# Four graph layers: copies of k, v and q of the next group ahead of the table copies, q requested behind the tables, output weights loaded during the sums

## What is computed

```python
def _typed_matmul(x, W, node_type):                 # one weight matrix per node type (4 types)
    all_t = jnp.einsum('ni,tio->tno', x, W)
    return all_t[node_type, jnp.arange(x.shape[0])]
k = _typed_matmul(h, k_linears, node_type).reshape(n, N_HEADS, D_K)      # 4 heads of 64
q = _typed_matmul(h, q_linears, node_type).reshape(n, N_HEADS, D_K)
v = _typed_matmul(h, v_linears, node_type).reshape(n, N_HEADS, D_K)
q_att = jnp.einsum('nhd,rhde->rnhe', q, relation_att)                    # 8 relations
v_msg = jnp.einsum('nhd,rhde->rnhe', v, relation_msg)
attn_score = jnp.sum(q_att[etype, col_idx] * k[row_idx], axis=-1)
score = attn_score * (relation_pri[etype] / SQRT_DK)
...
agg = jax.ops.segment_sum(alpha[..., None] * v_msg[etype, row_idx], col_idx, num_segments=n)
out = _typed_matmul(agg, a_linears, node_type)
out = jax.nn.sigmoid(skip)[node_type][:, None] * out
```

## Time and profile before

| | |
|---|---|
| time, median of 3 runs | 4174.1 us (4173.09 to 4183.92) |
| profiled execution, its own time | 4177.06 us |
| span of that execution | 4175.2 us |
| busy: PE, DVE, ACT, POOL | 75%, 54%, 21%, 66% |
| mean granted TensorE clock | 0.846 |
| group loop of the tables | about 1686 to 1936 |
| edges, first gather | 1952 |
| output, first instruction | 2966 |

### The profile page before, as it was taken

One profiled execution on the slowest core, in us unless ns is written; L12 is line 12 of the kernel. 1 busy time (PEld: TensorE's weight loads), 2 busy tenths in 40 slices (PEclk: granted clock), 3 DMA queues, 4 the chain that ended last, 5 costly groups with the idle time before them and its releaser, 6 DMA issues. The chain is left out here.

```text
span 4175.2 us, 64203 instructions
## 1 busy us (share of the span) xinstructions
PE 3149.1 (75%) x11666; PEld 2153.8 (52%) x11666; DVE 2234.4 (54%) x7572; ACT 894.9 (21%) x2584; POOL 2743.4 (66%) x2879
## 2 busy tenths in 40 slices
PE   5999938777788873786788878888786776767763
PEld 2444426556566652333667767777544444444442
DVE  8200037666666646333788868776654433444435
ACT  1333300000200000342344456555320000100000
POOL 3777767777677775234777767777217777477774
PEclk9999959999999986998887769877888877788876
DMA  4333323333333334566555546555213333333332
GB/s 142 142 145 151 142 73 105 106 105 105 95 105 106 106 107 131 217 257 233 165 165 165 164 129 176 163 162 162 66 50 106 105 105 106 99 106 105 105 106 90
DMA packets 226896, 540.00 MB, mean 129 GB/s; under 512 B 73482, under 2 KB 107948, under 8 KB 212876
## 3 DMA queue, kind: packets, MB, share of 16 engines
q0 software_dynamic: 136528, 374.97, 30.1%
q1 hardware_dynamic: 57880, 103.46, 6.8%
q10 hardware_dynamic: 32164, 57.91, 4.7%
HBM read 390.04 MB, written 146.09 MB: 128 GB/s over the span
## 5 line engine op out<-in xcount | busy, mean ns | idle before, releaser
L604 POOL DMA_INDIRECT gcn_edges_g<-table,rows_i x782 | 740.3, 947 | 434.3 <-ACTq L875 196.7
L923 PE MATMUL ps<-gcn_edges_g,gcn_edges_onehot 128*128 x1760 | 627.8, 497 | 309.1 <-SPq L620 271.4
L969 DVE TENSOR_TENSOR acc<-acc,ps 128x256 f32 (+1 forms) x880 | 370.0, 420 | 750.6 <-PE ps L923 740.3
L923 PEld LDWEIGHTS ps<-gcn_edges_g,gcn_edges_onehot 128*128 128x128 f32 x1760 | 392.2, 242 | 537.3 <-issue 484.5
L307 POOL DMA_INDIRECT records<-rec,slots x391 | 375.9, 961 | 184.1 <-issue 124.2
L604 POOL DMA_INDIRECT score_g<-table8v,rows_i x391 | 380.2, 972 | 131.0 <-issue 110.6
L604 POOL DMA_INDIRECT rel_g<-table,rows_i x391 | 371.8, 951 | 134.7 <-issue 96.9
L604 POOL DMA_INDIRECT score_g<-table8k,rows_i x391 | 371.4, 950 | 135.0 <-issue 109.4
L604 POOL DMA_INDIRECT conv_edges_g<-table,rows_i x391 | 371.7, 951 | 127.3 <-issue 93.8
L359 PE MATMUL ps<-w,xt 128*128 128x512 f32 x1000 | 435.8, 595 | 18.3 <-ACT xt L329 18.3
L1047 PE MATMUL ps<-q,onehot_t 128*128 x880 | 322.8, 503 | 109.6 <-DVE onehot_t L1146 108.3
(11 more groups left out here) (319 smaller groups left out, 4768.6 us busy)
## 6 DMA issues: line engine op xcount, KB each, us to landing
table<-tb SPq DMA_DIRECT2D x50, 1280.0 KB, 4.5
score_dst_bc<-dst_rows ACTq DMA_DIRECT2D x110, 256.0 KB, 3.5
sum_dst_bc<-dst_rows ACTq DMA_DIRECT2D x110, 256.0 KB, 3.4
gcn_edges_g<-table,rows_i POOLq DMA_INDIRECT x782, 2.8
table<-gcn_tb SPq DMA_DIRECT2D x50, 128.0 KB, 1.7
records<-rec,slots POOLq DMA_INDIRECT x391
rel_g<-table,rows_i POOLq DMA_INDIRECT x391, 2.8
conv_edges_g<-table,rows_i POOLq DMA_INDIRECT x391, 2.8
```

The source lines that it names most:

```text
L604: pool.indirect_dma_start(out=m.g[:, 2 * slot_of(p) + j, 0:D], out_offset=None, in_=table, in_offset=bass.IndirectOffsetOnAxis(ap=m.rows_i ...
L923: mm = pe.matmul(bank(m, i % BANKS, 0, width), m.onehot[:, 2 * k + j, :], window(m.g, slot + j, 0, width), start=(j == 0), stop=(j == 1))
L969: nc.vector.tensor_tensor(acc, acc, bank(m, i % BANKS, 0, width), ALU.add).then_inc(added, 1)
```

## The change

In `attention_tables`, ACT copies k and v of group i+1 before its table copies of group i, and `pick(i+2)` moves behind the kvt copy of i. DVE copies q of group i+1 before its table copies of group i. `pick` waits for a part of `xs` only when it comes to the first group that may need it. The read of `q_rows` is issued after both tables have landed; SP doesn't wait for it, PE does, at the start of the edges. The output weights are read into `m.q` by SP between the scores and the sums of the edges; `w_a` and its load in the output stage are gone, and PE reads the weights from `m.q`.

```diff
@@ attention_scores, tensor
         regs = ItemRegisters(pe, m, "score")
+        pe.wait_ge(m.q_back, 16)
         for i in range(total):
@@ attention_edges
             scores[0](sp)
+            sp.wait_ge(q_spread, ITEMS)
+            for ty in range(NTYPES):
+                sp.dma_start(m.q[:, 0:2 * NTYPES, :].rearrange("p (k t) d -> p k t d", t=NTYPES)[:, :, ty, :],
+                             a.a_lin[ty].rearrange("(k p) d -> p k d", p=P)).then_inc(m.out_weights, 16)
             sums[0](sp)
@@ attention_tables, sync
+            for j in (0, 1):
+                sp.wait_ge(stored[j], 16 * G)
             for b in (0, 1):
                 sp.wait_ge(q_slots[b], 16 * (G // 2))
-            sp.dma_start(m.q[:, 0:NT, :], m.q_rows[0:ROWS, :].rearrange("(t p) d -> p t d", p=P)).then_inc(q_stored, 16)
-            sp.wait_ge(q_stored, 16)
-            for j in (0, 1):
-                sp.wait_ge(stored[j], 16 * G)
+            sp.dma_start(m.q[:, 0:NT, :], m.q_rows[0:ROWS, :].rearrange("(t p) d -> p t d", p=P)).then_inc(m.q_back, 16)
@@ attention_tables, scalar
             def pick(i):
                 if i < G:
+                    if i < NT and i % PART == 0:
+                        act.wait_ge(back[i // PART], 16)
                     ...
+            def keep_kv(i):
+                if i < G:
+                    act.wait_ge(typed, i + 1)
+                    if i >= 2:
+                        act.wait_ge(kv_turned, i - 1)
+                    copy(kv[:, i % 2, :], bank(m, 1, 0, 512)).then_inc(kv_ready, 1)
...
-            for b in range(5):
-                act.wait_ge(back[b], 16)
             pick(0)
             pick(1)
+            keep_kv(0)
             for i in range(G):
-                pick(i + 2)
-                load(i + 3)
-                act.wait_ge(typed, i + 1)
-                if i >= 2:
-                    act.wait_ge(kv_turned, i - 1)
-                copy(kv[:, i % 2, :], bank(m, 1, 0, 512)).then_inc(kv_ready, 1)
                 act.wait_ge(kv_turned, i + 1)
                 if i >= 2:
                     act.wait_ge(product, 8 * (i - 1))
                 copy(kvt[:, i % 2, :, :], bank(m, 3, 0, 512).rearrange("p (c n) -> p c n", c=4)).then_inc(kvt_ready, 1)
+                pick(i + 2)
+                load(i + 3)
+                keep_kv(i + 1)
                 to_table(act, copy, i, 1, odd)
@@ attention_tables, vector
+            keep_q(0)
             for i in range(G):
-                dve.wait_ge(typed, i + 1)
-                if i >= 2:
-                    dve.wait_ge(q_slots[i % 2], 16 * (i // 2))
-                nc.vector.tensor_copy(qs[:, i % 2, :], bank(m, 2, 0, D)).then_inc(q_ready, 1)
+                keep_q(i + 1)
@@ attention_output
-        w = sb("w_a", [P, 2, NTYPES * D])
...
-            for ty in range(NTYPES):
-                sp.dma_start(w[:, :, ty * D:(ty + 1) * D], a.a_lin[ty].rearrange("(k p) d -> p k d", p=P)).then_inc(weights_in, 16)
...
-            pe.wait_ge(weights_in, 16 * NTYPES)
+            pe.wait_ge(m.out_weights, 16 * NTYPES)
...
-                        mm = pe.matmul(bank(m, 2 + 2 * (t % 2) + n, 0, 512), xt[:, t % 2, k, :], w[:, k, n * 512:(n + 1) * 512],
+                        mm = pe.matmul(bank(m, 2 + 2 * (t % 2) + n, 0, 512), xt[:, t % 2, k, :],
+                                       m.q[:, NTYPES * k + 2 * n:NTYPES * k + 2 * n + 2, :].rearrange("p t d -> p (t d)"),
```

More of the change, by code:

```diff
@@ L1230, in vector @@
         wins.free()
-    return (sync, gpsimd, tensor, scalar, vector), gather[1], maxed
+    return (sync, gpsimd, tensor, scalar, vector), gather[1], maxed, q_spread
 def attention_sum(ctx, nc, m, scores_released, maxed):
@@ L1368, in attention_sum, with attention_edges @@
     return sync, gpsimd, tensor, scalar, vector
-def attention_edges(nc, m):
+def attention_edges(nc, m, a):
     with ExitStack() as ctx:
-        scores, scores_released, maxed = attention_scores(ctx, nc, m)
+        scores, scores_released, maxed, q_spread = attention_scores(ctx, nc, m)
         sums = attention_sum(ctx, nc, m, scores_released, maxed)
@@ L1709, in attention_tables @@
          marks_flat, marks_found, into_ready, rel_ready, picked, turned, xt_ready, typed, kv_ready, q_ready, kv_turned, kvt_ready,
-         product, even, odd, att_turned, q_stored) = sems(
+         product, even, odd, att_turned) = sems(
             ctx, nc, "att", "weights_in", "rel_in", "chain", "dis_summed", "dis_rooted", "joined", "back0", "back1",
             "back2", "back3", "back4", "marks_turned", "marks_flat", "marks_found", "into_ready", "rel_ready", "picked", "turned",
-            "xt_ready", "typed", "kv_ready", "q_ready", "kv_turned", "kvt_ready", "product", "even", "odd", "att_turned",
-            "q_stored")
+            "xt_ready", "typed", "kv_ready", "q_ready", "kv_turned", "kvt_ready", "product", "even", "odd", "att_turned")
         placed, stored, q_slots = m.placed, m.stored, m.q_slots
@@ L1718, in attention_tables @@
                     marks_found, into_ready, rel_ready, picked, turned, xt_ready, typed, kv_ready, q_ready, kv_turned, kvt_ready,
-                    product, even, odd, att_turned, q_stored]
+                    product, even, odd, att_turned]
         block = ctx.enter_context(nc.Block())
@@ L1956, in columns, with keep_q @@
                 nc.vector.tensor_copy(xt[:, i % 2, :, :], bank(m, 0, 0, D).rearrange("p (k n) -> p k n", k=2)).then_inc(xt_ready, 1)
+            def keep_q(i):
+                if i < G:
+                    dve.wait_ge(typed, i + 1)
+                    if i >= 2:
+                        dve.wait_ge(q_slots[i % 2], 16 * (i // 2))
+                    nc.vector.tensor_copy(qs[:, i % 2, :], bank(m, 2, 0, D)).then_inc(q_ready, 1)
             columns(0)
             columns(1)
+            keep_q(0)
             for i in range(G):
-                dve.wait_ge(typed, i + 1)
-                if i >= 2:
-                    dve.wait_ge(q_slots[i % 2], 16 * (i // 2))
-                nc.vector.tensor_copy(qs[:, i % 2, :], bank(m, 2, 0, D)).then_inc(q_ready, 1)
+                keep_q(i + 1)
                 if i + 2 < G:
@@ L1984, in attention_output @@
         tmp = sb("tmp8", [P, 2, NTYPES - 1, D])
-        weights_in, small_in, types_zero, chain, exp_ready, divided, turned, xt_ready, product, emptied, own, kept = sems(
-            ctx, nc, "out", "weights_in", "small_in", "types_zero", "chain", "exp_ready", "divided", "turned", "xt_ready",
+        small_in, types_zero, chain, exp_ready, divided, turned, xt_ready, product, emptied, own, kept = sems(
+            ctx, nc, "out", "small_in", "types_zero", "chain", "exp_ready", "divided", "turned", "xt_ready",
             "product", "emptied", "own", "kept")
-        m.spent += [weights_in, small_in, types_zero, chain, exp_ready, divided, turned, xt_ready, product, emptied, own, kept]
+        m.spent += [small_in, types_zero, chain, exp_ready, divided, turned, xt_ready, product, emptied, own, kept]
         norm = TileNorm(ctx, nc, m, "att")
@@ L2172, in four_graph_layers @@
         m.scattered = sems(ctx, nc, "all", "scattered0", "scattered1")
-        m.marked, m.placed = sems(ctx, nc, "all", "marked", "placed")
+        m.marked, m.placed, m.q_back, m.out_weights = sems(ctx, nc, "all", "marked", "placed", "q_back", "out_weights")
         m.stored = sems(ctx, nc, "all", "stored_k", "stored_v")
@@ L2240, in four_graph_layers @@
         m.scores = c5.enter_context(nc.sbuf_tensor("scores", [P, ITEMS, 2 * HEADS], F32))
-        attention_edges(nc, m)
+        attention_edges(nc, m, a)
         with ExitStack() as c2:
```

## The result

| | before | changed |
|---|---|---|
| median of the runs, both kernels on one chip | 4173.6 us (4 runs, 4168.78 to 4183.92) | 4120.05 us (4 runs, 4118.11 to 4122.4) |
| profiled execution: time, span | 4177.06, 4175.2 us | 4122.4, 4120.6 us |
| mean granted TensorE clock | 0.846 | 0.848 |

The changed kernel takes 0.9869 of the time before, 95% interval 0.9857 to 0.9881: 53.5 us less. The forecast was 4106 us, 68 less.

The account below looks back on a forecast made before the run. A chain of waits was taken to bound the table loop, POOL's gathers the edges. 46.7 + 7.6 + 9.4 + 4.8 = 68.5 us off 4177.1 gave 4108.6, 4106 us as a median; range 4098 to 4128.

Parts of the forecast that it names:

- Loop: Table loop: kv and q copied ahead of the table copies cut the period from 8.93 to 7.2 us, 46.7 us less.
- then one more pair, whose length is the distance of two table copies, 0.86 us: Table loop, last part of PE's own ring: 3.39 + 2.83 us, then this pair, sum 7.08 us.
- a slack of 1.7 us: Table loop: ACT's spare time before PE wants kvt at 7.08 us, said to swallow most slow landings, up to 7.0 us.
- falls behind k: Table loop: v copies waiting for their slot drop behind k until v's landing shortens; v settles near 7.08, not 7.44 us.
- Start of the loop: Before the table loop: the first pick waits only for the first part of `xs`, 7.6 us less.
- Seam: Tables to edges: the last v table ends the block instead of q, 10.8 us earlier, some given back, 9.4 us less.
- q late: Start of the edges: PE starts 11 to 18 us behind POOL's first gather, made up later, cost 0.
- Output weights: Output stage: with weights loaded early, ACT's 4.83 us idle before xt goes, 4.8 us less.
- The stores: Rival, table loop: stores become the bound, period some 8 us, 25 us in place of 46.7, time 4128; chance 0.12.
- The clock: Rival, table loop: granted clock falls to 1.2 GHz, PE's ring doubles to 14.2 us, time 4294; chance 0.03.
- q too late: Rival, edges: PE and DVE aren't caught up when the scores end, sums begin 10 us late, time 4116; chance 0.05.
- a loop that doesn't shorten: Rival, table loop: another wait at the old place leaves 8.9 us, only the seams' 22 us count, 4152; chance 0.05.

Follow-up runs that it names:

- The two slots: The changed kernel with a second slot for each table, in `m.q`, each with its own semaphore; ratio 0.9882, on a second chip 4119.35 us, ratio 0.9854.

## Why the prediction was right or wrong

The sign, the mechanism of the loop and the range (4098 to 4128) held; the end of the block at the seam was read wrong in part. The point was 14 us too low, and two terms make up 13.3 of them. That the time still lies inside the forecast's own 4101 to 4122 is partly luck: both terms came out below their own bounds, while the start took its best value and the output term got 3.2 us from a granted clock that nobody had forecast.

**Loop: 36.6 us for 46.7.** The chain was read rightly: without the order the loop is 240.5 us, with it alone 203.0. The failed step is "then one more pair, whose length is the distance of two table copies, 0.86 us". The rows after have 1767.17 - 1766.11 = 1.06 us there. Of the 0.20 us between them, 0.10 is PE going from 64 rows to 128. The other 0.10 is that 1763.79, where the 2.83 us end, is the start of a weight load that ran 0.11 us ahead of its product. PE's ring is 7.28, not 7.08, and the best end of my bracket could not be reached. The 0.20 us are 27 x 0.20 = 5.4 us of the 10.1. Before, the edge from 64 rows to 128 could not be read, because PE waited for kv behind it: a phase that ends in a wait hides its own cost.

The other part is slow landings. I let a slack of 1.7 us "swallow most of them". The mean period is 203.99 / 27 = 7.56 us, of which 0.28 is waits for slots, where I had 0.12: another 27 x 0.16 = 4.3 us. (The last 0.5 us is the period before, 240.58 / 27 = 8.91 on the mean where one group had shown 8.93.) Fifteen of the 27 periods are 7.28; four are 7.6 to 7.7, and three are 8.6 to 8.8, among them the one shown. These three alone bring 4.4 of the 7.4 us above 27 x 7.28. A k table that lands in 6.5 us uses up the slack and delays v's copies behind it. The two slots took these waits away: 7.0 us.

The medians of the landings stayed at 4.5 us for k and 5.2 for v in the loop, so by them the v slot's ring is still the 7.44 that I worked out, above PE's 7.28. That v "falls behind k" is what the 40 waits for v show, counted on both engines, of about 1.2 us each. The Trainium skill's page "DMA: Bandwidth & Descriptors" (anatomy of one DMA, SWDGE path) gives a fixed 2.0 us and the bytes by 436 GB/s, an estimate of 4.4 us for a table. The trace agrees for k, issued first (4.5). It has 5.2 for v, issued 1.9 us behind k, and 6.5 and 7.2 for single ones, and these decide here.

**Start of the loop: 7.7 us for 7.6.** The first read landed by 4.77 us after its issue, near the shortest of the five before.

**Seam: 6.2 us for 9.4.** The failed step is "SP ended the block when q had landed", and with it "Now the last v table ends it: 1935.04 + 5.2". POOL's DRAIN ended at 1951.27, 0.2 us behind q, so two chains were last together. The DRAIN was that long because the last v table, taken at 5.2 us, needed 11.7 beside the read of q; 4.49 us behind its landing the DRAIN ended. Taking SP's wait away and leaving the read where it was would have brought little or nothing, an estimate from these two ends. Moving the read behind the table brought the rest: the table lands in 4.5 us, and the DRAIN ends 9.90 us behind its start. Then 10.80 us pass from the last table to the first gather. Added to the 1935.04 of the earlier trace rows they give 1945.84, 6.3 us before 1952.18. The 1.0 us that I had given back for the last group was 0.2 (8.60 us for 8.42 from the last `turn_back` to the v table). In the terms of the forecast: I asked what is late next in the loop, and didn't ask it at the seam.

**q late: no cost, as said.** q landed 14.8 us after its issue; PE began 8.9 us behind POOL's first gather, not 11 to 18, since that gather was itself later than I thought. The gathers' stretch stayed at 1001 us. Beginning q later still, in the edges, put PE 20 us behind, and the stretch showed no loss: 1001.5 us against 1003.3 of the changed kernel on the same chip.

**Output weights: 6.6 us for 4.8, by the marks.** xt starts 5.26 us after `rden` in place of 10.22, 5.0 us less. The first product copied out by DVE comes only 3.4 us earlier: the first eight products of PE take 6.44 us in place of 4.86, at a mean granted clock of 0.57, so mostly at the lower level (0.50, 1.2 GHz). PE had stood idle for 2.93 us before them; with the loads late there is no such pause. The view by windows has the clock of those products after and before:

```profile
2922.80:2929.30 6.50, 6.47 (x10) 2.84 (x11) 1.21 (x6) 0.26 (x1) 0.00 (x0) 0.57 0.00 0
```

```profile
2975.60:2981.70 6.10, 6.02 (x14) 3.00 (x15) 0.01 (x1) 0.77 (x2) 0.00 (x0) 0.71 0.00 1
```

From 2929.3 on it is 1.00. In the nine executions with the weights early the eight products took 4.88 to 6.44 us, six of them 6.0 or more; in the three with the weights late, 4.83 to 5.06. So the early start mostly, but not always, gives back some 1.2 us here, on a term that I had priced by ACT's wait alone.

The other 3.2 us of the 6.6 aren't the weights' doing as far as the traces show. From the first product on everything in the stage stands 3.4 us earlier; only at its end does the distance grow. The windows below begin 110 us behind the first product copied out and end at the next layer's first gather. They hold the same instructions, before in 15.7 us and after in 12.5:

```profile
3091.70:3107.40 15.70, 8.68 (x25) 5.54 (x23) 4.60 (x16) 3.76 (x10) 0.00 (x0) 0.61 0.12 42
```

```profile
3039.30:3051.80 12.50, 5.45 (x25) 3.70 (x23) 4.63 (x16) 3.77 (x10) 0.00 (x0) 0.98 0.15 53
```

PE had been busy without a gap at 1.00 until shortly before these windows, then its work thinned (busy for 3.39 of 5.2 us before, 3.14 of 5.0 after). Before, the granted clock fell to the lower level (0.50) at 3095.2; after, it was still 1.00 at 3051. The second run of the changed kernel had its first product 4.6 us earlier and a last window like the one before (clock 0.62), hence 4.8 and not 6.6. In the seven traces whose first eight products took 5.8 us or more the clock stayed up to the end, or nearly; in the five with 5.1 or less it fell as before. Why is not shown.

**The rivals.** The stores are not the bound: DMA share 0.72, and with two slots the period fell to PE's with the share at 0.75. Still, a part of what the rival spoke of is there, the slow landings. The clock stayed at 1.00 in the loop. q too late, and a loop that doesn't shorten, are out by the marks.

## What to carry to other kernels

When a wait is taken out of a chain, work out what is late next at every place where the time is counted, block ends too: what a block waited for may have hidden an engine's own tail, here a DRAIN of POOL's queue that ended 0.2 us behind it. Here a read beside the last store had lengthened that tail too. An engine's ring that is read from a trace in which it waits lacks what the wait covers; take the ring as a lower bound and look for the same hand-over, here 64 rows to 128, in another stretch where it runs without a pause. Add the ring up from the starts of the products, not of the weight loads, which run ahead by different amounts. Read a busy engine by its work rows, not by the idle time of its weight loads: these wait ahead of products that are still running.

## What the hardware showed that I had not expected

- POOL's first gather of the edges came 10.80 to 10.91 us after the start of its last indirect DMA of the tables, in six runs that no read of q held up, whether SP had work in between or not; with two table slots it was 11.0 to 11.2 us in four runs. A DRAIN of POOL's queue fills this time. It ended 9.90 us behind the start of the last table that landed in 4.5 us, and 4.49 us behind the landing of one that took 5.6 to 11.7.
- The last v table took 11.7 us to land beside the read of q, and 4.5 us without it.
- PE's way from transposes of 128 rows to products of 64 rows and back adds 0.20 us to the products, 0.10 us at each edge. At the end of the products the next load starts 0.76 us after the last one (`[0.76 <-issue]`), within the products 0.24 us. The page "TensorE: Matmul & The Clock Gate" of the Trainium skill (Part 3, the mechanism) says that a weight load runs beside products in flight only when it goes to other rows of the array. (It names a background weight buffer as another case.) The traces don't agree with the "only": in `by_type`, where every load and every product goes to all 128 rows, a load of the changed kernel starts at 1761.25 and lasts 0.19 us, beside a product that starts with it and is followed by the next one at 1761.46.
- Idle time of the weight-load rows of 0.56 us, released by DVE, stood for 0.25 us of PE's time at most.
